# Second layer's gate by rows: the state held stationary, W_h streamed, the result turned by VectorE

## The reference, cut to what matters

```python
# layer 1, a gated recurrence; x1 = x + h(t) goes on
z = sigmoid(xzt + h @ U_z + vz)
r = sigmoid(xrt + h @ U_r + vr)
hh = tanh(xht + r * h @ U + vh)
h = (1.0 - z) * h + z * hh
# layer 2, the one that the change touches; z_t is x1 of that step
leak = 1.0 - alpha                       # alpha: one value per feature
gate = sigmoid(h @ Wh.T + z_t @ Wz.T + b)
h = tanh(h * leak + gate * z_t)          # x2 = x1 + h
# layers 3 and 4: per-feature gates with cumulative sums, then a low-rank adapter
```

## Time and profile before

| | before |
|---|---|
| median of 3 runs | 979.05 us (978.9 to 980.17) |
| the profiled execution: time, span | 979.33 us, 977.5 us |
| TensorE matmuls busy | 938.2 us (96%) |
| TensorE loads busy | 768.3 us (79%) |
| VectorE busy | 850.6 us (87%), 2882 instructions |
| ScalarE busy | 601.4 us (62%) |
| GpSimd busy | 216.7 us (22%) |
| the 256 time steps | from about 20 to about 602 us |

### The profile page before, as it was taken

The page is one execution under the profiler, slowest core; times in us unless marked ns, Lnnn a source line. Parts: engine busy times, 40 slices in busy tenths (PEclk is TensorE's granted clock), DMA queues, the critical chain, the costliest instruction groups (busy, mean ns, idle before and its releaser), DMA issues.

```text
span 977.5 us, 104703 instructions
## 1 busy us (share of the span) xinstructions
PE 938.2 (96%) x46862; PEld 768.3 (79%) x46862; DVE 850.6 (87%) x2882; ACT 601.4 (62%) x2607; POOL 216.7 (22%) x430
## 2 busy tenths in 40 slices
PE   6799999999999999999999999969999999999996
PEld 6799999999999999999999997335555555555554
DVE  3588888888888888888888887799999999999993
ACT  3577767767777777777777775335455556555552
POOL 0011111111111111111111111324334334433340
PEclk7999999999999999999999999979999999999999
DMA  5031330330100101001001000100010000001001
GB/s 178 24 99 50 121 112 24 123 111 24 38 24 24 38 24 35 27 27 35 27 24 38 24 27 9 28 0 26 24 41 32 24 24 24 24 24 47 25 25 43
DMA packets 38006, 41.48 MB, mean 42 GB/s; under 512 B 5088, under 2 KB 31200, under 8 KB 36832
## 3 DMA queue, kind: packets, MB, share of 16 engines
q1 hardware_dynamic: 36832, 40.55, 13.2%
q10 hardware_dynamic: 1152, 0.66, 0.2%
HBM read 32.28 MB, written 8.91 MB: 42 GB/s over the span
## 4 chain that ended last, share of the span: by engine, by line
PE 61%; DVE 29%; issue 7%; DMA 2%; ACT 1%; ACTq 0%; DVEq 0%
PE bank L826 26%; PE bank L757 18%; PE bank L772 13%; DVE arena L690 11%; DVE early L709 4%; DVE early L700 4%; DVE early L713 2%; DVE early L707 2%; DVE early L688 2%; DVE early L694 2%; DMA x_ahead<-in_x 1%; PE bank L934 1%; DMA beta<-in_beta 1%; PE bank L905 1%; PE bank L951 1%
## 5 line engine op out<-in xcount | busy, mean ns | idle before, releaser
L288 POOL TENSOR_TENSOR x<-x_f,h_f 128x64 f32 x256 | 84.1, 329 | 524.9 <-PE bank L826 523.8
L934 PE MATMUL bank<-x,wl 128*128 (+1 forms) x384 | 181.3, 611 | 0.9 <-DVE rank_rows L667 0.9
L757 PE MATMUL bank<-x_ahead,early 128*32 128x64 f32 x8256 | 173.6, 221 | 3.1 <-ACT bank L361 2.2
L772 PE MATMUL bank<-early,none_h 128*32 128x64 f32 x4096 | 167.3, 223 | 3.0 <-issue 3.0
L402 ACT ACTIVATE cand_kept<-bank 128x32 f32<-128x32 f32 x512 | 99.4, 203 | 92.3 <-PE bank L826 92.3
L826 PE MATMUL bank<-none_h,early 128*32 128x32 f32 x8192 | 150.3, 196 | 3.3
L622 DVE TENSOR_TENSOR_SCAN none_h<-zero_z,cand_kept 128x64 f32<-128x64 f32 x512 | 122.6, 282 | 30.7 <-ACT cand_kept L402 3.3
L757 PEld LDWEIGHTS bank<-x_ahead,early 128*32 128x32 f32 x8256 | 142.1, 110 | 4.0 <-issue 2.3
L826 PE MATMUL bank<-h_f,early 128*32 128x32 f32 x8288 | 140.5, 203 | 4.0 <-issue 3.0
L826 PEld LDWEIGHTS bank<-none_h,early 128*32 128x32 f32 x8192 | 131.3, 111 | 13.1 <-DVE none_h L622 12.9
L826 PE MATMUL bank<-rh_f,early 128*32 128x32 f32 x8192 | 140.5, 201 | 0.9 <-issue 0.5
(11 more groups left out here) (103 smaller groups left out, 1528.1 us busy)
## 6 DMA issues: line engine op xcount, KB each, us to landing
x_ahead<-in_x SPq DMA_DIRECT2D x130, 64.0 KB, 1.8
x_in<-in_x SPq DMA_DIRECT2D x32, 256.0 KB, 2.6
arena<-in_w SPq DMA_DIRECT2D x8, 1024.0 KB, 6.8
out<-y SPq DMA_DIRECT2D x32, 256.0 KB, 2.4
rank_rows<-in_bias_rows SPq DMA_DIRECT2D x1, 1024.0 KB, 6.7
arena<-scratch SPq DMA_DIRECT2D x64, 16.0 KB
early<-in_cx SPq DMA_DIRECT2D x1, 768.0 KB, 4.4
early<-in_wx SPq DMA_DIRECT2D x1, 768.0 KB, 6.5
```

The lines of the kernel that those rows point to most:

```text
L288: pool.tensor_tensor(x2[:, :, :, s], x1_f[:, u % LOOP], h1_f[:, u % 2], ALU.add).then_inc(x2_done, 1)
L757: mm = pe.matmul(out[32 * j:32 * j + 32], weights(k, j, m), moving(k), start=False, stop=False, tile_position=(0, 32 * j), skip_group_chec ...
L772: mm = pe.matmul(out[32 * j:32 * j + 32], moving(k), weights(k, j), start=False, stop=False, tile_position=(0, 32 * j), skip_group_check=True)
L934: mm = pe.matmul(banks[(at + 2 * par) % 4][:], wl2[:, k, mat, unit], x2[:, k, bass.ds(p * GB, GB), :].rearrange("p q t -> p (q t)"), start ...
```

## The change

Layer 2's gate is computed in row layout. The W_h product takes 8 matmuls in place of 16: the state is stationary and 64 columns of W_h move. The input product with W_z is also by rows, with the same number of matmuls as before (16 for two steps). ScalarE writes the sigmoid in row layout to `gate_rows`, and VectorE turns it back with one transpose. The product h * leak is an instruction of its own over both halves, placed between the transpose and gate * x1; `keep1` holds the leak value repeated over the batch. The sum is then one addition over both halves. The bias seed of the gate comes from `bias_rows`, as it does for z.

```diff
-        seed_g = sb("seed_g", [P, HALVES, STEPS, B])
+        seed_g = sb("seed_g", [P, STEPS, SLAB])
+        gate_rows = sb("gate_rows", [P, 2, SLAB])
+        kept1_f = sb("kept1_f", [P, HALVES, B])
-        pre_g = [half(banks[6 + n]) for n in range(2)]
+        pre_g = [rows_of(banks[6 + n]) for n in range(2)]
 ...
# ScalarE
-                act.activation(gate_f[:], pre_g[(s // STEPS) % 2][:, :, s % STEPS, :], ACT.Sigmoid).then_inc(gate_done, 1)
+                act.activation(gate_rows[:, s % 2], pre_g[(s // STEPS) % 2][:, s % STEPS], ACT.Sigmoid).then_inc(gate_done, 1)
 ...
# VectorE
-            for m in range(HALVES):
-                dve.tensor_copy(seed_g[:, m], *repeated(seed_g[:, m], bias_f[:, 3, m:m + 1])).then_inc(seeds_ready, 1)
+            for v in range(STEPS):
+                dve.tensor_copy(seed_g[:, v], bias_rows[:, 3]).then_inc(seeds_ready, 1)
 ...
             def second_gated(n, u):
                 s = n * BODY + u - LAG
                 dve.wait_ge(gate_done, s + 1)
+                dve.transpose(gate_f[:].rearrange("p m b -> p (m b)"), gate_rows[:, (u - LAG) % 2]
+                              ).then_inc(gate_turned, 1)
+                dve.tensor_tensor(kept1_f[:], h1_f[:, (u - LAG + 1) % 2], keep1[:], ALU.mult).then_inc(gx_done, 1)
+                dve.wait_ge(gate_turned, s + 1)
                 dve.tensor_tensor(gx_f[:], gate_f[:], x1_f[:, (u - LAG) % LOOP], ALU.mult).then_inc(gx_done, 1)
 
             def second_sum(n, u):
                 s, at = n * BODY + u - LAG, (u - LAG) % 2
-                dve.wait_ge(gx_done, s + 1)
-                for m in range(HALVES):
-                    new = dve.scalar_tensor_tensor(h1_pre[:, at, m], h1_f[:, 1 - at, m], keep1[:, m, 0:1], gx_f[:, m],
-                                                   ALU.mult, ALU.add)
-                new.then_inc(pre1_done, 1)
+                dve.wait_ge(gx_done, 2 * (s + 1))
+                dve.tensor_tensor(h1_pre[:, at], kept1_f[:], gx_f[:], ALU.add).then_inc(pre1_done, 1)
 ...
# TensorE
             def ahead_second(at, par):
-                for m in range(HALVES):
-                    mm = ahead(pre_g[par][:, m].rearrange("p v b -> p (v b)"), m, col(wz1),
-                               lambda k: x1_f[:, at:at + STEPS, k, :])
+                for v in range(STEPS):
+                    mm = by_rows(pre_g[par][:, v, :], lambda k: x1_f[:, at + v, k, :], lambda k, j: wz1[:, k, j, :])
                 return mm
 ...
-                gate = lambda k, m: quarter(pre_g[(s // STEPS) % 2][:, m, s % STEPS, :], col(wh1),
-                                            lambda k: h1_f[:, (s - 1) % 2, k], k, m)
+                gate = lambda k: by_rows(pre_g[(s // STEPS) % 2][:, s % STEPS, :], lambda k: h1_f[:, (s - 1) % 2, k],
+                                         lambda k, j: wh1[:, k, j, :], (k,))
                 pe.wait_ge(h1_done, 1)
                 if sums:
                     pe.wait_ge(pre1_done, sums)
-                gate(0, 0).then_inc(h1_done, -1)
-                gate(0, 1)
-                gate(1, 0)
-                gate(1, 1).then_inc(gate_pre, 1)
+                gate(0).then_inc(h1_done, -1)
+                gate(1).then_inc(gate_pre, 1)
```

More of the change, by code:

```diff
@@ L158, in build_program @@
             sem("zero_done"), sem("rh_done"), sem("kept_done"), sem("h_done"), sem("x1_done"))
-        gx_done, pre1_done, x2_done = (
-            sem("gx_done"), sem("pre1_done"), sem("x2_done"))
+        gate_turned, gx_done, pre1_done, x2_done = (
+            sem("gate_turned"), sem("gx_done"), sem("pre1_done"), sem("x2_done"))
         ln_step, std_done, ada_done, hid_pre, hid_done = (
@@ L367, in seed_gate @@
             def seed_gate(par):
-                act.activation(flat(pre_g[par]), flat(seed_g[:]), ACT.Copy).then_inc(seeded, 1)
+                act.activation(pre_g[par].rearrange("p v e -> p (v e)"), seed_g[:].rearrange("p v e -> p (v e)"),
+                               ACT.Copy).then_inc(seeded, 1)
             act.wait_ge(table_in, 1)
```

## The result

The changed kernel takes 963.69 us (median of 4 runs, 963.24 to 966.66), the kernel before 978.97 (4 runs, 978.52 to 980.17): a ratio of 0.9848, with an interval of 0.9827 to 0.987. Run again later, it took 965.09 (0.9866, interval 0.9846 to 0.9886). The prediction was 962.0. The profiled execution took 964.07 us with a span of 962.3, so the span is 15.2 shorter.

A forecast was written before the change was run, and what follows sets the result against it. TensorE, the dependent chain and VectorE meet within hundredths in ordinary steps; TensorE alone is late in a turn's first. Per turn 3 x 0.04 + 0.15 = 0.27, times 64 = 17.3 us: 979.3 - 17.3 = 962.0, range 955 to 980.

The forecast's parts named there:

- Part 1: TensorE, layer 2's gate block, every step: 16 matmuls become 8, block 0.36 to 0.21 us, saving 0.15 (0.04 to 0.18).
- Part 2: TensorE, W_z product by rows, 16 matmuls for 16: no change, bounds 0 to 0.05 us per two steps either way.
- Part 3: VectorE: transpose at 0.42 after the scan, gate * x1 at 0.79, sum at 1.04, r*h possible at 1.18; costs nothing.
- Part 4: Gain per four-step turn: 0.04 us in each of three ordinary steps, 0.15 in the first; 0.27, times 64 is 17.3.
- the gates' second part starts at 0.53: TensorE, ordinary step: gate loads needing the state's half 1 start at 0.53 after the scan, not 0.56 to 0.58; gain 0.04.
- rival D: TensorE saves 0.18 and gates run in a burst behind their new stall: 0.39 us a turn, 954 us; chance 0.10.
- The 0.3: Behind the loop: the last three layer-2 steps take 0.1 us more each on VectorE, 0.3 us in all.
- A: VectorE's block about 0.1 us longer eats the ordinary steps' gain, r*h at 1.28 to 1.31: 975 to 981; chance 0.15.
- B: VectorE becomes the bound, r*h at 1.41, 0.33 us a turn slower: 1000 us; decides from about 1.31; chance 0.10.
- C: TensorE's gate block doesn't shrink, only 0.04 us saved, a turn gains 0.04 to 0.16: 969 to 977; chance 0.15.

The follow-up runs named there:

- the kernels with two and with four more matmuls: Changed kernel plus two or four matmuls of 64 columns, results unread, between the halves of layer 2's gate block: 975.51 and 975.33 us.
- the old sum: Changed kernel with the leak product put back into two half-width sums; gate by rows and transpose stay: 979.08 us, ratio 1.0005.
- the kernel with six more: Changed kernel plus six matmuls of 64 columns, results unread, between the halves of layer 2's gate block: 1013.16 us, ratio 1.0349.
- VectorE's half alone: Kernel before with only the separate leak product and the sum as one addition; gate stays in feature layout, no transpose: 979.71 us, ratio 1.0000.

## Why the prediction was right, and where two of its terms were off

**Part 1, right.** The block was to go from 0.36 to 0.21; it is 0.20. In the first step of a turn the gates start at 0.57 for 0.70. The Trainium skill ("TensorE: Matmul & The Clock Gate", Wait — 56ns, not 53.3ns?) has 2.5 ns over the columns for each matmul, and by that next to nothing would have been saved. The trace agrees with it for blocks that run in a burst (7.4 ns a record of 32 columns, 0.56 of the 13.1 of 64), not for the block that was replaced, which took 11.3 ns a record. The same section of the Trainium skill also has a floor of about 25 ns from start to start for small matmuls, which the prediction left out. An estimate from that page's figures is then 16 x 29.2 ns against 32 x 25, a ratio of 0.58. Measured is 0.20 / 0.36 = 0.56. But a burst record holds its tile for 4 x 7.4 = 30 ns, so no run here shows that floor at work. What was saved is in the main the difference between 11.3 ns and the 7.4 of the bursts.

**Part 2, right.** The input block from `x_f` is 0.52 long before (402.18) and after (405.27).

**Part 3, VectorE, right in kind and 0.11 too careful.** Turned at 0.39 (predicted 0.42), gate * x1 at 0.67 (0.79) and 0.22 long (0.22), sum at 0.93 (1.04), VectorE free for r*h at 1.07 (1.18). The mis-sized term is the 0.37 from a transpose to the instruction that waits for it, read from L607 to L612. The dependence alone is 0.28 here (403.75 to 404.03). In the 0.37 the product in between held VectorE for 0.19, by the prediction's own reading, where the leak product holds it for 0.11 (403.92 to 404.03). The error did no harm, since r decides: r*h starts at 1.12, 0.23 after r's sigmoid.

**Part 4, the sum right, its terms not.** I had 3 x 0.04 + 0.15 = 0.27 for a turn. Measured is 3 x 0.07 + 0.055 = 0.265. That the two errors, 0.09 too little and 0.095 too much, cancel is luck. Over the loop that is 192 x 0.07 + 64 x 0.055 = 17 us, beside the 16.1 of its 251 steps after the first four.

- The ordinary step gained 0.07, not 0.04. The failed step is "the gates' second part starts at 0.53": I reckoned with where it starts, and left the rate at which it then runs as it was. By the medians over the ordinary steps it did start at 0.53 (0.57 before), a gain of 0.04 as forecast, but its 24 loads then come at 7.5 ns each, where they took 10.0 before. That is another 0.06 at the last load, of which some 0.03 reaches r. This was rival D's mechanism, and the kernels with two and with four more matmuls bear out its size: with most of the idle used up, the loads are back at 9.9 ns, and 0.05 of the 0.07 is gone. That a queue fills during the idle stretch stays my reading. Idle time alone doesn't make the burst: in a turn's first step, behind a wait of 0.23, the first 22 loads of the gates' second part take 0.28, which is (0.28 - 0.11) / 21 = 8.1 ns each.
- The first step of a turn gained 0.055 in the mean, not 0.15. Where nothing else is late it gained 0.10. Timeline of such a step:

```profile
416.26 0.48 DVE L625 TENSOR_TENSOR_SCAN none_h<-zero_z,cand_kept 128x64 f32<-128x64 f32 x2
...
416.83 0.16 PEld L829 LDWEIGHTS bank<-none_h,early 128*32 128x32 f32 x8 [0.23 <-DVE none_h L625]
...
417.41 0.36 ACT L394 ACTIVATE r_f<-bank 128x32 f32<-128x32 f32 x2 [0.42 <-PE bank L829]
417.64 0.35 DVE L605 TENSOR_TENSOR rh_f<-r_f,none_h 128x32 f32<-128x32 f32 x2 [0.22 <-ACT r_f L394]
...
418.61 0.48 DVE L625 TENSOR_TENSOR_SCAN none_h<-zero_z,cand_kept 128x64 f32<-128x64 f32 x2
```

The gates start 0.13 sooner than in the earlier trace rows by this count, r's sigmoid at 1.15 for 1.24, r*h at 1.38 for 1.48, the next scan at 2.35 for 2.45. So of 0.15 on TensorE 0.10 arrives. In the other three places of the 16-step pattern something else is about 0.10 late. The three, of the changed kernel's first execution: VectorE's transpose of z at 1.77 in place of 1.66 (a window of its own),

```profile
398.81 0.48 DVE L625 TENSOR_TENSOR_SCAN none_h<-zero_z,cand_kept 128x64 f32<-128x64 f32 x2
...
400.58 0.25 DVE L610 STREAM_TRANSPOSE zero_z<-z_rows 128x64 f32<-128x64 f32 x1
```

r*h 0.33 after r's sigmoid in place of 0.23, at the end of VectorE's own body,

```profile
408.70 0.36 ACT L394 ACTIVATE r_f<-bank 128x32 f32<-128x32 f32 x2 [0.42 <-PE bank L829]
409.03 0.31 DVE L605 TENSOR_TENSOR rh_f<-r_f,none_h 128x32 f32<-128x32 f32 x2 [0.32 <-ACT r_f L394]
```

and r's sigmoid itself, 0.68 behind the gates' first load in place of 0.58, after a pause of TensorE within the gates.

```profile
425.48 0.16 PEld L829 LDWEIGHTS bank<-none_h,early 128*32 128x32 f32 x8 [0.23 <-DVE none_h L625]
...
426.16 0.36 ACT L394 ACTIVATE r_f<-bank 128x32 f32<-128x32 f32 x2 [0.52 <-PE bank L829]
```

The kernel before has none of the three in its medians (2.45 in all four places); that its r, 0.09 later, covered them is a guess. With bodies of 8 steps on VectorE and ScalarE, the first steps in two of the four places are clean (2.35). The other two (2.38) follow a step in which the transpose of z is late (2.17 for 2.10). In them the gates start at 0.50, sooner than 0.57, r's sigmoid is 0.68 behind the gates' first load, and r*h is 0.28 behind the sigmoid in place of 0.23. So the late r*h goes with the end of VectorE's body, and the other two aren't TensorE's own loop alone. What makes them late stays open.

**Ahead of and behind the loop.** The 3.1 us gained in the first four steps and the 3.7 us lost behind the loop were in no term. They cancel to a loss of 0.6, and that is luck too: without the first the profiled execution would have been at 967.2, without the second at 960.4. The 0.3 that I had put behind the loop for VectorE's work can't be told apart within it.

**The rivals.** A, VectorE's block eats the ordinary gain, is what happens with the old sum: 979.1, within A's 975 to 981. Its price was set a little high, though: r*h at 1.26 was enough for it, where I had 1.28 to 1.31. B, slower, needed r*h beyond 1.31, and none of its ends was met: the gate is sooner, GpSimd is out of the way, and the sum holds VectorE by 0.14 (in the kernel with six more, from the sum at 402.00 to r*h at 402.14). C, the block doesn't shrink, is out by the 0.20. The stated range, 955 to 980, took in C and part of A as well, so that the time fell into it says little; the 0.20 and the new idle say more. D gave the ordinary steps their 0.07, but the first steps don't have its 0.18. The Trainium skill ("SBUF — State Buffer", Who interferes with whom) speaks of VectorE and GpSimd excluding each other. In VectorE's half alone that falls on the leak product, 0.30 long. In the changed kernel GpSimd's addition (403.63 to 403.96) lies over the transpose, which is 0.24 long there and 0.25 elsewhere, and hardly over the products.

## What to carry to other kernels

Where two engines become ready within hundredths of each other, price a saving on one together with the other's free time: here each half of the change was worth 0 within 0.2%, and both were worth 1.5%. An idle stretch ahead of a block on TensorE isn't always slack: here the loads behind it came at 7.5 instead of 10.0 ns, and filling most of that stretch cost 0.05 us a step. Small matmuls on column tiles were paid here by the round over the tiles, not by their number. Before unrolling a body, estimate its code in bytes: here a body of about 180 KB, an estimate from the instruction queue, was fetched on each pass. And before comparing whole times, look ahead of and behind the loop: a stall that came and went with unrelated edits moved them by up to 5 us.

## What the runs showed of the hardware

- A loop body of TensorE that no longer stays on the chip: 8 steps in place of 4 made 0.16 MB of instructions 5.85 MB, with stalls of 0.6 to 4.4 us (median 1.8), and the kernel 1.75 times as long. If the 5.85 MB are 32 passes, the two bodies are about 90 and 180 KB (an estimate); no size in between was tried.
- A matmul of 64 moving columns on each of four column tiles costs TensorE about 0.11 us (0.31 - 0.20), and on two of the four the kernel takes as long (975.3 and 975.5 us; the next block's last load 0.11 and 0.08 later).
- Records of 32 columns: 7.4 ns each behind an idle stretch of 0.12 us, 9.5 with hardly one, 11.3 in steady issue. A record of 64 columns takes 13.1, so halving the number of records saves little against the 7.4 (14.8 for two) and much against the 11.3 (22.6).
- A stall of 2.9 to 3.3 us in straight-line code behind the loop, in four of nine traces (the body of 8 steps aside) and in none with more matmuls. In the changed kernel it cost not only itself but the granted clock (0.50 for 6.8 us, from within the stall on), about 5.4 us in all (21.1 for 15.7).
